# Norm, turned bias and reordered weights of the first attention made inside the convolution's block

## What is computed

```python
x = L0_conv(x)   # non-local block: softmax(theta^T phi) over pooled pixels, 1x1 convs, batch norm, + x
x = L1_conv(x)   # 1x1, depthwise 3x3, 3x3, 1x1 convs on quantised weights and activations, + x, relu
# then on tokens (8 batches, 256 tokens, 256 channels), 16 heads of 16:
x = x + attn(layernorm(x))          # causal, ALiBi bias, w_in with b_in: q, k, v = split(xn @ w_in + b_in)
x = x + xn @ ternary(weight)        # xn = layernorm(x)
x = x + attn(layernorm(x))          # second attention, no bias
x = x + experts(layernorm(x))       # router over 8 experts, top 2
```

## Time and profile before

| | |
|---|---|
| median of 3 runs (lowest to highest) | 663.61 us (662.3 to 663.61) |
| profiled execution: its time, its span | 662.7 us, 660.9 us |
| busy: TensorE, VectorE, ScalarE, POOL | 91%, 68%, 50%, 18% of the span |
| granted TensorE clock, mean | 0.966 |
| last VectorE instruction of the first block | starts 111.9 us |
| first T of the second block | starts 116.77 us |

### The profile page before, as it was taken

One profiled execution on the slowest core, in us unless ns is written; L12 is line 12 of the kernel. 1 busy time (PEld: TensorE's weight loads), 2 busy tenths in 40 slices (PEclk: granted clock), 3 DMA queues, 4 the chain that ended last, 5 costly groups with the idle time before them and its releaser, 6 DMA issues.

```text
span 660.9 us, 11320 instructions
## 1 busy us (share of the span) xinstructions
PE 599.0 (91%) x4224; PEld 408.0 (62%) x4224; DVE 446.4 (68%) x1273; ACT 327.8 (50%) x552; POOL 117.7 (18%) x115
## 2 busy tenths in 40 slices
PE   9884875868999999999999979999999999999897
PEld 4743433646777777777767757576575756565443
DVE  4768857757577577577577584876768576776464
ACT  2436677617656666566566553353443535353110
POOL 2121000260323313303203302011030200000000
PEclk9886899888999999999999989999999999999999
DMA  9500000475225224234134132214050220000000
GB/s 337 217 0 0 1 0 11 95 209 155 74 76 148 70 81 148 59 91 144 50 96 144 41 105 77 69 40 120 0 150 11 74 87 17 1 17 1 16 15 17
DMA packets 40254, 50.66 MB, mean 77 GB/s; under 512 B 4052, under 2 KB 33492, under 8 KB 39892
## 3 DMA queue, kind: packets, MB, share of 16 engines
q1 hardware_dynamic: 40200, 49.94, 24.7%
HBM read 35.11 MB, written 14.68 MB: 75 GB/s over the span
## 4 chain that ended last, share of the span: by engine, by line
PE 61%; DVE 15%; issue 2%; ACT 2%; DMA 1%; SPq 1%; POOL 0%; DVEq 0%; ACTq 0%
PE ps L1264 14%; PE ps L1147 8%; PE ps L1139 7%; PE ps L1221 5%; PE ps L1210 5%; DVE nmax L1431 4%; PE ps L1131 4%; PE ps L1206 3%; PE ps L1190 3%; PE ps L1228 2%; DVE acc L1511 2%; PE ps L1185 2%; PE ps L1182 2%; PE ps L1180 2%; DVE xn L1387 2%
## 5 line engine op out<-in xcount | busy, mean ns | idle before, releaser
L1431 DVE TENSOR_REDUCE nmax<-ps 128x2 f32<-128x512 f32 (+1 forms) x192 | 130.8, 687 | 78.7 <-PE ps L1190 50.6
L1324 ACT ACTIVATE PT<-ps 128x512 f32<-128x512 f32 x192 | 113.2, 597 | 116.2 <-PE ps L1210 114.6
L1264 PE MATMUL ps<-wm,xnT 128*128 128x512 f32 x256 | 119.9, 599 | 0.7
L1091 POOL TENSOR_TENSOR rstd<-ve,fix 128x2 f32<-128x2 f32 x32 | 22.2, 693 | 321.5 <-DVE ve L1382 321.5
L1318 ACT ACTIVATE QS<-ps 8x1024 bf16<-8x1024 f32 x64 | 65.0, 1016 | 27.2 <-PE ps L1195 25.2
L1210 PE MATMUL ps<-QS,KS 110*128 110x256 bf16 (+3 forms) x512 | 74.7, 247 | 0.0
L1511 DVE SCALAR_TENSOR_TENSOR acc<-ps,gate,acc 128x256 f32<-128x256 f32 x128 | 61.6, 481 | 18.5 <-PE ps L1264 16.2
L1264 PEld LDWEIGHTS ps<-wm,xnT 128*128 128x128 f32 x256 | 45.1, 190 | 39.7 <-issue 38.1
L1139 PE MATMUL ps<-xnT,by_dim 128*128 128x256 f32 x256 | 62.6, 391 | 2.2 <-ACT xnT L1289 2.2
L1111 POOL TENSOR_TENSOR parts<-rest,fix 128x512 bf16<-128x512 f32 x30 | 38.1, 1268 | 138.4 <-DVE rest L1400 100.2
L1206 PE MATMUL ps<-fixb 128*128 128x256 bf16 (+1 forms) x192 | 60.1, 313 | 2.3 <-DVE nmax L1431 2.0
(11 more groups left out here) (215 smaller groups left out, 948.5 us busy)
## 6 DMA issues: line engine op xcount, KB each, us to landing
parts_dram<-parts SPq DMA_DIRECT2D x32, 384.0 KB, 3.1
QS<-parts_dram SPq DMA_DIRECT2D x96, 128.0 KB
KS<-parts_dram SPq DMA_DIRECT2D x96, 128.0 KB, 2.6
wt<-wt_dram SPq DMA_DIRECT2D x1, 2562.0 KB, 19.6
wm<-wm_dram SPq DMA_DIRECT2D x1, 2449.0 KB, 13.2
xc<-x_dram SPq DMA_DIRECT2D x8, 256.0 KB, 5.5
out_dram<-res SPq DMA_DIRECT2D x8, 256.0 KB, 2.1
w<-w_dram SPq DMA_DIRECT2D x1, 845.0 KB, 7.8
```

Source lines behind the costliest of these rows:

```text
L1264: mm = pe.matmul(d, normT(stage, batch)[:, c, t * P:(t + 1) * P], M("We", c * EXPERTS * CH + e * 2 * CH, 2 * CH), start=(c == 0), stop=(c ...
L1324: act.activation(PT[:, pt_slot(piece, n), :], bank(piece), ACT.Exp).then_inc(drain(piece), 1)
L1431: dve.tensor_reduce(group[:, 0, :] if part == 0 else group[:, 1, 2 * part - 2:2 * part], bank(piece).rearrange("p (j n) -> p j n", n=w_), ...
```

## The change

The norm of the first batch (the pieces LNa and LNb of stage 0, batch 0) is left out of the piece order and its instructions stand at the end of the first block: VectorE's statistics between the last L935 and L938, POOL's power at the end of POOL's list, `xn` after L938. The turned bias is made in the first block: the reordered identity before the ternary sum, TensorE's bias matmul before its ones matmul (into the same PSUM bank 1, columns 4 to 7, instead of bank 7), the two `qk_bias` operations before the ternary scale. TensorE waits for them before the fourth z matmul, which overwrites the bank. `turn_by_dim(act, 0)` stands in ScalarE's list behind `expert_folded(2)`. The buffers `xn`, `stats`, `mv`, `ve`, `rstd`, `qk_bias` and `ident_by_dim` live through both blocks now. The second block's lists start with the pieces at once.

```diff
@@ in_order
         for k, (kind, stage, n, step) in enumerate(FLOW[s] + ((("PAD", 0, 0, -18),) if at == 0 else ())):
+            if at == 0 and stage == 0 and kind in ("LNa", "LNb"):
+                continue
@@ first block, gpsimd
                 add_x(1, 2)
 
+                pool.wait_ge(first_var, 1)
+                pool.tensor_tensor(rstd[:, 0], ve[:, 0], F("minus_half"), ALU.pow).then_inc(first_rstd, 1)
@@ first block, tensor
                 fold_expert(2)
                 pe.wait_ge(tern_summed, 1)
+                pe.wait_ge(by_dim_ready, 1)
+                both = WT["bq0"][0]
+                pe.matmul(ps[:, 1, 4:4 + 2 * NC2], ident_by_dim[:], wt[:, both:both + 2 * NC2], start=True, stop=True)\
+                  .then_inc(bias_turned, 1)
                 pe.matmul(ps[:, 1, 0:1], F("ones"), tern_sum[:], start=True, stop=True).then_inc(tern_summed, 1)
...
                         if o == 0 and q == 3:
+                            pe.wait_ge(prepared, 2)
                             pe.wait_ge(tern_scaled, 1)
@@ first block, scalar
                 expert_folded(2)
+                act.wait_ge(wt_loaded, 16)
+                turn_by_dim(act, 0)
                 for o in range(NC2):
@@ first block, vector
+                dve.tensor_copy(ident_by_dim[:].rearrange("p (d h) -> p d h", d=DH),
+                                F("ident").rearrange("p (h d) -> p d h", d=DH)).then_inc(by_dim_ready, 1)
                 dve.wait_ge(wt_loaded, 16)
                 dve.tensor_reduce(tern_sum[:], T("tern"), AX.X, ALU.add, apply_absolute_value=True)\
                    .then_inc(tern_summed, 1)
+                dve.wait_ge(bias_turned, 1)
                 dve.wait_ge(tern_summed, 2)
+                dve.tensor_scalar(qk_bias[:, 0], ps[:, 1, 4:4 + NC2], DH ** -0.5, None, ALU.mult).then_inc(prepared, 1)
+                dve.tensor_copy(qk_bias[:, 1], ps[:, 1, 4 + NC2:4 + 2 * NC2]).then_inc(prepared, 1)
...
+                dve.wait_ge(tok_out_act, 1)
+                for t in range(2):
+                    op = dve.bn_stats(stats[:, 0, t, :], X[:, t, :])
+                settle(op)
+                dve.memset(ve[:, 0], EPS)
+                for t in range(2):
+                    op = dve.bn_aggr(mv[:, 0, t, :], stats[:, 0, t, :])
+                settle(op)
+                dve.tensor_tensor(ve[:, 0], ve[:, 0], mv[:, 0, :, 1], ALU.add).then_inc(first_var, 1)
                 dve.wait_ge(tok_done, 8)
                 dve.tensor_scalar(X[:, 14:16, :].rearrange("p a n -> p (a n)"), ps[:, 3, :], 0.0, None, ALU.max)\
                    .then_inc(tok_out_dve, 1)
+                dve.wait_ge(first_rstd, 1)
+                for t in range(2):
+                    dve.tensor_scalar(xn[:, 0, t, :], X[:, t, :], mv[:, 0, t, 0:1], rstd[:, 0, t:t + 1],
+                                      ALU.subtract, ALU.mult)
@@ second block: tensor, scalar, vector
-                    pe.wait_ge(prepared, 1)
-                    both = WT["bq0"][0]
-                    pe.matmul(ps[:, 7, 0:2 * NC2], ident_by_dim[:], wt[:, both:both + 2 * NC2], start=True, stop=True)\
-                      .then_inc(bias_turned, 1)
...
-                    act.wait_ge(wt_loaded, 16)
-                    turn_by_dim(act, 0)
-                    act.wait_ge(prepared, 3)
...
-                    dve.wait_ge(wt_loaded, 16)
-                    dve.tensor_copy(ident_by_dim[:].rearrange("p (d h) -> p d h", d=DH),
-                                    F("ident").rearrange("p (h d) -> p d h", d=DH)).then_inc(prepared, 1)
-                    dve.wait_ge(bias_turned, 1)
-                    dve.tensor_scalar(qk_bias[:, 0], ps[:, 7, 0:NC2], DH ** -0.5, None, ALU.mult).then_inc(prepared, 1)
-                    dve.tensor_copy(qk_bias[:, 1], ps[:, 7, NC2:2 * NC2]).then_inc(prepared, 1)
-                    dve.wait_ge(prepared, 3)
```

More of the change, by code:

```diff
@@ L253, in build, with turn_by_dim @@
         folded = sem("folded")
+        prepared = sem("prepared")
+        bias_turned = sem("bias_turned")
+        by_dim_ready = sem("by_dim_ready")
+        first_var = sem("first_var")
+        first_rstd = sem("first_rstd")
+        xn = sb("xn", [P, 2, 2, CH])
+        stats = sb("stats", [P, 2, 2, 6])
+        mv = sb("mv", [P, 2, 2, 2])
+        ve = sb("ve", [P, 2, 2])
+        rstd = sb("rstd", [P, 2, 2])
+        qk_bias = sb("qk_bias", [P, 2, NC2])
+        ident_by_dim = sb("ident_by_dim", [P, P])
+        def turn_by_dim(act, m):
+            by_head = T(("in0", "in1")[m]).rearrange("p (c k o h d) -> p c k o h d", c=NC2, k=3, o=NC2, h=P // DH)
+            for k, scale in enumerate((DH ** -0.5, 1.0)):
+                for o in range(NC2):
+                    act.activation(by_dim[:, m, k, :, o].rearrange("p c (d h) -> p c d h", d=DH),
+                                   by_head[:, :, k, o].rearrange("p c h d -> p c d h"),
+                                   ACT.Copy, scale=scale).then_inc(turned_by_dim, 1)
         with ExitStack() as c1:
@@ L946, in lb @@
                 return sb(name, shape, dt, c2)
-            xn = lb("xn", [P, 2, 2, CH])
             xnT = lb("xnT", [P, 2, NC2, PIX])
@@ L953, in build @@
             spare = lb("spare", [P, 1])
[L954 to L959, removed]
             rest = lb("rest", [P, 2, NC2, PIX])
@@ L980, in build @@
             sems = {name: sem(name) for name in COUNTS.total}
-            prepared = sem("prepared")
-            bias_turned = sem("bias_turned")
             bias_loaded = sem("bias_loaded")
@@ L1271, in tensor_piece @@
                     mm.then_inc(sems[f"bank_full{COUNTS.bank[piece]}"], 1)
[L1274 to L1281, removed]
             def scalar_piece(act, piece):
```

## The result

| | before | after |
|---|---|---|
| median of 20 runs each | 661.54 us | 657.8 us |
| lowest to highest | 658.98 to 663.61 | 655.9 to 659.75 |
| profiled execution: span, mean granted clock | 660.9, 0.966 | 655.6, 0.973 |
| ratio after / before, 95% interval | | 0.995 (0.9939 to 0.996) |

The change makes the kernel 3.3 us faster by the ratio (2.6 to 4.0), 3.7 by the medians; 3.09 had been worked out.

What follows compares the result with a forecast made beforehand. One serial chain at the join of the two blocks was taken as the bound. Q's drain (-3.29) plus the bias matmul (+0.20) gave -3.09, so 659.6 or 660.5 by base; forecast 660.1 us, range 658.3 to 662.2.

Steps and rivals of the forecast that it cites:

- What bounds: At the join of the two blocks, one serial chain from 112.9 to about 125 sets when the dense part starts.
- Edit 1: Norm of batch 0 into the first block's tail: that block ends 0.94 us later, T starts 2.91 earlier.
- Rival (a): First block's tail: L938 and POOL's pow exclude each other, chain 0.65 later; -2.44, 660.8 us; chance 0.10.
- Edit 2: Bias and identity into the convolution: VectorE's work hidden there, TensorE's bias matmul costs 0.20 us before z.
- Edit 3: turn_by_dim's 2.20 us on ScalarE moved behind the third fold copy: hidden in idle time, needed for the norm's move.
- What is late next: Second block's start: `chosen`, then ScalarE's PAD copy, hold Q's drain whatever Q's clock; drain 3.29 us earlier.
- Sum: Whole kernel: -3.29 for Q's drain plus 0.20 for the bias matmul gives -3.09 us.
- The level: Whole kernel's absolute time: 660.1 us, between 659.6 from the profiled execution and 660.5 from the median of runs shown.
- rival (b): At Q's drain: chain follows Q's matmuls, not PAD's copy, and the clock stays high; -4.9, 658.3 us; chance 0.06.
- (c): Join not shortened, later work such as SyncE's loads eats the gain: below 1.3 us, 662 to 663; chance 0.12.
- (d): TensorE-bound work: low-clock stretches cover over 8.8 us more, so the change loses; 665.7 with two more stretches; chance 0.04.

Runs made afterwards that it cites:

- the run again: The changed kernel, unaltered, measured once more beside the kernel before on one chip: median 657.02 us, ratio to before 0.9933.
- edits 2 and 3 alone: Against the kernel before: bias, identity and reordered weights moved into the first block, the norm left at the join; ratio 0.9971.
- edit 1 alone: Against the kernel before: the norm in the first block's tail; bias, identity and turn_by_dim left at the join; ratio 0.9976.
- The second group: The unaltered changed kernel against before, measured again on one chip: medians 657.02 and 661.77 us, ratio 0.9933.
- the experiments on PAD: Changed kernel with ScalarE's PAD copy doubled (0.9989), late (0.9989), late with late memsets (0.9981), in quarters (0.9967), in quarters with late memsets (0.997); ratios to before.
- with the memsets late too: Changed kernel with the PAD copy behind K's drain, its SyncE copies later, and VectorE's memsets behind K's split of batch 1; ratio to before 0.9981.

## Why the prediction was right and wrong, point by point

- **What bounds.** Right. The chain at the join was the place, and every change to it showed at the first M.
- **Edit 1.** Right to 0.15. Stats to POOL's start 1.31 (1.32), pow beside L988. The tail was to be longer by 0.94: from the start of the first residual addition to VectorE's first instruction in the second block it is 7.56 before (105.36 to 112.92), 8.42 after (103.71 to 112.13) and 8.36 in the run again, so 0.86 and 0.80 more. In the first of these the pow was over 0.1 before `xn` started, and L988 had waited 0.28 for TensorE, whose transposes began at the low clock (0.75 at 103 to 107); in the run again L988 did not wait. Rival (a) is out: the pow started 0.20 before L988 in one profile and 0.03 after it in the other, and both had their usual length. The Trainium skill's page VectorE: DVE Perf Modes (Mode 2×_2P) asks for operands in SBUF, and L988 reads PSUM; its 0.69 beside the pow agrees.
- **Edit 2.** The matmul cost 0.23: from its start at 35.63 to z at 36.00 is 0.37, where before the ones matmul alone took 0.14. I had taken 0.20. VectorE's part was hidden, as said; but the claim that the copy ahead of the ternary sum is hidden holds only while TensorE is slow here. From the start of y to z it is 7.09 with the edit and 6.87 without at the low clock (changed kernel again, before), 0.22 more; at the high clock 4.76 and 4.35 (edits 2 and 3 alone, edit 1 alone), 0.41 more, with TensorE idle 0.37 and 0.19 for the ternary sum.
- **Edit 3.** Right: hidden in the convolution (ScalarE idle 4.34 before z's affine), and needed: left at the join it costs 1.2 (3.14 - 1.97).
- **What is late next.** Right: `chosen` 1.26 plus 0.16 after the block's start, PAD's copy, Q's drain at 5.09 against 5.11 worked out, with a fast and with a slow Q.
- **Sum.** -3.09 worked out, -3.14 and -2.98 in the fill (-3.22 and -3.12 with the tails as measured), and 3.3 (2.6 to 4.0) over the run. The second group gives 0.9933 (3.4 to 5.6 us), whose lower end lies above 3.09. The surplus by the medians of the twenty runs is 0.65, by the ratio 0.2. Part of it could be the 6 us less at the low clock; no run tests that, and what T at the high clock gives is already in the sum (3.29 against 2.93). Where the surplus comes from stays open.
- **The level.** Here is the step that failed. "I predict between them: 660.1" rested on three runs and a profiled one, all of 662.3 or more, so that before stood at 663.2 in the sum; it measured 661.54 in the twenty runs beside the changed kernel and 661.2 over 100. Of the 2.3 us between 660.1 and 657.8 this base is 1.65 and the surplus over the sum the other 0.65. With 661.54 the same sum gives 658.45, just inside the range; with 661.2 it gives 658.1, just outside. "The runs of before differ by 1.3 among themselves" took the spread of three for the spread of the kernel; it is 5.2 over 100. The range got its lower end from rival (b), which the runs rule out for this kernel, and nothing for the place of the base. It missed by 0.5 us.
- **Rivals (c) and (d).** (c) is out as a whole: the loads kept what was won. But the experiments on PAD show its mechanism one step further on: with the memsets late too, 1.7 us were won at Q's drain, batch 1's store left only 0.5 earlier than in the first profile, and its slow landing took that and more. (d): low stretches got shorter in sum, not longer, and the dense start's was there in both kernels.

## What to carry to other kernels

Work out an edit's effect as a difference in one execution, but take the level and its spread from as many runs as there are; three runs within 1.3 us stood at one end of a spread of 5. Before moving a step out of the way of a chain, look at what the queue holds behind it: ScalarE's constant fill was the next bound, doubling it cost its full length at the first M, and moving it made it the head of the next batch's chain. An operation that covers another hides that one's variation (Q at 1.8 or 3.6 behind the PAD copy's 3.61), which appears when the first is moved.

## What the runs showed of the hardware

By its mean granted clock TensorE was at 1.2 GHz for 35 and 31 us in two executions of the same program, and for 45 us in the profile before. Of these, 6.9 lie at 391 to 399 (clock 0.57, TensorE busy 6.22 of 8 us), far from the change; the changed kernel run again had 1.00 there and was busy all 8 us. The store of batch 1's parts to DRAM landed in 2.72 to 2.96 us in nine profiles and in 4.02 to 5.08 in the five others with the same bytes, on the chain that feeds the first M.
